# Routed experts by sorted tiles in place of all experts dense, and native fp32 attention projections, in an AdaLN attention and mixture-of-experts block

## The chip, the cores and the metric

The kernel runs on one core of a Trainium2 chip. The metric is the device time of one execution in microseconds. A core has five engines that run side by side, each through its own list of instructions in order, and that wait for each other on semaphores: TensorE (PE, matrix products into PSUM, the weight load shown apart as PEld), VectorE (DVE), ScalarE (ACT), GpSimd (POOL) and SyncE (SP, which here only issues DMAs). Sixteen DMA engines move data between DRAM and SBUF.

## The reference

There are 8 batches of 1024 tokens with 128 features, all fp32. `mod` holds six vectors of 128 for each batch, made from a condition.

```python
h = layernorm(x) * (1 + ca) + sa
q, k, v, g = h @ Wq.T, h @ Wk.T, h @ Wv.T, h @ Wg.T      # 8 heads of 16
q, k = rope(q), rope(k)
kv = einsum('bshd,bshe->bhde', k, v)
num = einsum('bshd,bhde->bshe', q, kv) * scale + v.sum(1)
den = einsum('bshd,bhd->bsh', q, k.sum(1)) * scale + 1024
x = x + ga * (((num / den + conv5(v)) * g) @ Wo.T)
h = layernorm(x) * (1 + cb) + sb
probs = softmax((h @ Wgate + bg) / 5.0)                    # 8 experts
gates = the two largest of probs, each over their sum
out_e = gelu(h @ W1[e] + b1[e]) @ W2[e] + b2[e]            # 128 -> 256 -> 128
x = x + gb * sum_e gates[e] * out_e
```

## The kernel before

Batches are independent. A batch passes through a list of stages (`STAGES`, laid out by `TICK`): norm, transposes of x (`xT`), projections (`qkv`), transposes of v, q and of the inverse denominators, convolution, `gate`, `out`, second norm, `x1T`, `logit`. Its routing follows in `LATE`. Then its experts run as 16 units, one for each half of 512 tokens and each of the 8 experts: every token goes through every expert, and the gate is zero for the six that were not chosen. The schedule has 16 ticks a batch. In each tick one unit of batch f stands beside stages of batch f+1, and every engine walks through the same list (`schedule`, `tick`), so what an engine does next is written out beforehand. The middle six batches are one loop of three rounds with two batches each.

One unit is this chain. `layer1` (L471 to L473): six products 128x128 by 128x512, since each fp32 product is split into three float32r products (`split`: high by high, low by high, high by low). ScalarE applies gelu in PSUM (L702). VectorE multiplies by the gates, which were spread over all partitions through DRAM (L1019). ScalarE rounds to the high part (L709). GpSimd subtracts it for the low part (L807). `layer2` (L592 to L594): six products that accumulate in `ps_y` over all experts. The qkv and gate projections are split in the same way, and their low parts come from GpSimd (L771). `normalise` is L846, the transposes L466, the native fp32 products L502 (kv), L514 (den), L519 (num), L543 (out) and L558 (logit). The bias b2 is one product at L587. SyncE loads x, brings the gates to DRAM and back spread (L400 to L420) and stores y (L428).

## Time and profile before

| | |
|---|---|
| median of 3 runs | 706.93 us (705.43 to 3041.11) |
| span of the profiled execution | 704.5 us |
| PE busy | 590.6 us, 84% |
| PEld busy | 473.8 us, 67% |
| DVE busy | 534.0 us, 76% |
| POOL busy | 450.5 us, 64% |
| ACT busy | 402.9 us, 57% |
| DMA moved | 47.57 MB, mean 68 GB/s |

In rows of groups, `out<-in (partitions x elements, type) xcount` is followed by the busy time in us and the mean ns of one, then by the idle time of the engine just before and what ended it. A native fp32 product has two records on PE, a float32r product or a transpose has one. PE records overlap (the next begins before the last ends), so the pace of a run of products is the distance between their starts. In rows of a stretch the columns are: from and to, length, busy time and number of instructions of PE, PEld, DVE, ACT and POOL, granted TensorE clock as a share of 2.4 GHz, DMA share, GB/s.

### The profile page before, as it was taken

The numbers are of one execution on the slowest core, as the hardware profiler recorded it, in microseconds if no ns is written. First come the engines' busy times: TensorE is split into PE (matmuls) and PEld (weight loads), VectorE is DVE, ScalarE is ACT, GpSimd is POOL, SyncE is SP. The second block draws the span as 40 slices with busy tenths as digits, with TensorE's granted clock in tenths as the row PEclk, the third lists the DMA queues.
The fourth block names the chain that finished last, engine by engine and source line by source line (L and its number), as shares of the span: only waits on it lengthen the run. The fifth ranks groups of instructions, "written<-read, shape, count | busy, mean of one in ns | idle before, by whom it ended". The sixth has DMA issues, their size and how long they took to land.

```text
span 704.5 us, 9302 instructions
## 1 busy us (share of the span) xinstructions
PE 590.6 (84%) x2750; PEld 473.8 (67%) x2750; DVE 534.0 (76%) x1029; ACT 402.9 (57%) x639; POOL 450.5 (64%) x311
## 2 busy tenths in 40 slices
PE   4823897799987988789987989879887989889996
PEld 3623775587776866678765867668665777667884
DVE  5686677977889678787789778796798877884442
ACT  2331565566565746656565746657556655765773
POOL 3372555685866936857667838569458666665885
PEclk9975798899999989989999989999999989998999
DMA  6000341035100441008010341004210180004300
GB/s 239 2 30 0 127 125 31 1 98 168 45 1 15 128 124 45 1 17 247 15 30 14 113 138 45 1 15 158 91 45 0 34 230 15 1 15 169 96 16 15
DMA packets 37682, 47.57 MB, mean 68 GB/s; under 512 B 2096, under 2 KB 20432, under 8 KB 37392
## 3 DMA queue, kind: packets, MB, share of 16 engines
q1 hardware_dynamic: 37216, 46.77, 21.8%
q10 hardware_dynamic: 432, 0.43, 0.2%
q14 instruction: 23, 0.19, 0.1%
q8 instruction: 11, 0.18, 0.1%
HBM read 42.21 MB, written 4.98 MB: 67 GB/s over the span
## 4 chain that ended last, share of the span: by engine, by line
PE 30%; POOL 24%; DVE 21%; issue 17%; ACT 5%; POOLq 1%; DMA 1%; DVEq 0%; SPq 0%; ACTq 0%
POOL hid_l L807 20%; PE ring L466 4%; PE ring L519 3%; DVE xn L846 3%; DVE conv L1005 3%; DVE stats L834 3%; PE ps_y L592 3%; PE ring L514 3%; PE ps_y L593 3%; PE ps_y L594 2%; PE ps_h L471 2%; PE ps_h L472 2%; PE ps_h L473 2%; PE ring L558 2%; DVE hid_g L1019 2%
## 5 line engine op out<-in xcount | busy, mean ns | idle before, releaser
L807 POOL TENSOR_TENSOR hid_l<-hid_g,hid_h 128x1024 fp32r<-128x1024 f32 x128 | 304.9, 2389 | 147.4 <-ACT hid_h L709 138.4
L702 ACT ACTIVATE ps_h<-ps_h,b_f 128x512 f32<-128x512 f32 x256 | 158.5, 658 | 109.0 <-PE ps_h L473 108.3
L1019 DVE TENSOR_TENSOR hid_g<-ps_h,spread 128x1024 f32<-128x1024 f32 x128 | 155.5, 1216 | 71.1 <-POOL hid_l L807 58.2
L709 ACT ACTIVATE hid_h<-hid_g 128x1024 fp32r<-128x1024 f32 x128 | 135.5, 1058 | 11.7 <-DVE hid_g L1019 11.7
L592 PE MATMUL ps_y<-hid_h,w_h 128*128 128x512 f32 x256 | 114.3, 446 | 2.4 <-POOL hid_l L807 2.4
L471 PE MATMUL ps_h<-h_h,w_h 128*128 128x512 f32 x256 | 105.4, 412 | 9.2 <-DVE hid_g L1019 9.2
L593 PE MATMUL ps_y<-hid_h,w_l 128*128 128x512 f32 x256 | 106.0, 414 | 0.0
L594 PE MATMUL ps_y<-hid_l,w_h 128*128 128x512 f32 x256 | 105.8, 413 | 0.0
L472 PE MATMUL ps_h<-h_h,w_l 128*128 128x512 f32 x256 | 102.4, 400 | 0.0
L473 PE MATMUL ps_h<-h_l,w_h 128*128 128x512 f32 x256 | 102.1, 399 | 0.0
L466 PE MATMUL ring<-consts_f,xn 128*128 128x128 f32 x128 | 27.7, 362 | 63.4 <-DVE xn L846 62.2
L466 PEld LDWEIGHTS ring<-consts_f,xn 128*128 128x128 f32 x128 | 19.1, 182 | 73.2 <-DVE xn L846 58.1
L471 PEld LDWEIGHTS ps_h<-h_h,w_h 128*128 128x128 f32 x256 | 49.7, 194 | 24.5 <-DVE hid_g L1019 13.6
L592 PEld LDWEIGHTS ps_y<-hid_h,w_h 128*128 128x128 f32 x256 | 52.9, 207 | 16.0 <-POOL hid_l L807 3.7
L593 PEld LDWEIGHTS ps_y<-hid_h,w_l 128*128 128x128 f32 x256 | 52.0, 203 | 12.8 <-issue 3.0
L594 PEld LDWEIGHTS ps_y<-hid_l,w_h 128*128 128x128 f32 x256 | 51.4, 201 | 12.5
L472 PEld LDWEIGHTS ps_h<-h_h,w_l 128*128 128x128 f32 x256 | 49.4, 193 | 11.1 <-issue 0.2
L473 PEld LDWEIGHTS ps_h<-h_l,w_h 128*128 128x128 f32 x256 | 48.8, 191 | 11.8
L846 DVE TENSOR_SCALAR xn<-x,mean_var,rstd 128x128 f32<-128x128 f32 x64 | 54.7, 924 | 0.1
L776 POOL TENSOR_TENSOR qk<-qk_cos,qk_sin 128x256 f32<-128x256 f32 x64 | 46.7, 746 | 8.5 <-DVE qk_sin L879 8.4
L771 POOL TENSOR_TENSOR h_l<-heads,h_h 128x512 fp32r<-128x512 f32 x16 | 20.6, 1289 | 43.4 <-ACT heads L641 43.2
L1009 DVE SCALAR_TENSOR_TENSOR conv<-v_t,lepe_f,conv 128x1024 f32<-128x1024 f32 x32 | 44.2, 1382 | 0.3
(127 smaller groups left out, 929.9 us busy)
## 6 DMA issues: line engine op xcount, KB each, us to landing
spread<-gates_dram SPq DMA_DIRECT2D x16, 2048.0 KB, 8.9
xs<-in_x SPq DMA_DIRECT2D x8, 512.0 KB, 3.9
out<-y SPq DMA_DIRECT2D x16, 256.0 KB, 2.3
spread<-in_w SPq DMA_DIRECT2D x2, 1024.0 KB, 6.8
gates_e<-parts_dram SPq DMA_DIRECT2D x24, 32.0 KB
ga<-ga_dram SPq DMA_DIRECT2D x1, 512.0 KB, 3.6
spread<-in_wmod SPq DMA_DIRECT2D x1, 384.0 KB, 5.1
spread<-in_wqkvg ACTq DMA_DIRECT2D x1, 256.0 KB, 5.3
```

Source lines behind the costliest of these rows:

```text
L466: last = pe.transpose(dst[:, j * P:(j + 1) * P], src(j), ident)
L471: pe.matmul(dst, wh, ah, start=True, stop=False)
L472: pe.matmul(dst, wl, ah, start=False, stop=False)
L473: return pe.matmul(dst, wh, al, start=False, stop=True)
L592: pe.matmul(ps_y[:, :], w2_h[:, e, g, :], high, start=False, stop=False)
L593: pe.matmul(ps_y[:, :], w2_l[:, e, g, :], high, start=False, stop=False)
L594: last = pe.matmul(ps_y[:, :], w2_h[:, e, g, :], low, start=False, stop=(e == E - 1 and g == HH - 1))
L702: last = act.activation(bank, bank, ACT.Gelu, bias=b1_f[:, e, g:g + 1])
L709: act.activation(hid_h[n % 4][:, :, :], hid_g[n % 2][:, :, :], ACT.Copy)\
L807: pool.tensor_tensor(hid_l[n % 4][:, :, :], hid_g[n % 2][:, :, :], hid_h[n % 4][:, :, :].bitcast(F32), ALU.subtract).then_inc(s_hl, 1)
L846: last = dve.tensor_scalar(xn[:, j, :], src[:, j, :], mean_var[:, j, 0:1], rstd[:, j:j + 1], ALU.subtract, ALU.mult)
L1019: dve.tensor_tensor(hid_g[n % 2][:, :, :], ps_h[n % HIDDEN][:, :, :], gates_all[c][:, e, :].unsqueeze(1).to_broadcast([P, HH, CT]), ALU.mu ...
```

## The change

The experts no longer run dense. For each batch VectorE picks the two experts of each token (`choose`, 13 steps), forms the gates (`soften`, 14 steps) and, with prefix sums from TensorE (nine small float32r products, `prefix`), the row at which each token's copy stands in a list sorted by expert, each expert padded to whole tiles of 128 rows (`put`, 11 steps). There are 2048 copies, and 23 tiles always suffice. GpSimd scatters the normalised rows to DRAM with 16 indirect DMAs of 128 rows (`scat`) and later gathers the results with 16 more (`gat`). SyncE reads each tile's expert number into a register (`value_load`), loads that expert's whole weights for each of the 23 tiles (128 rows of 514 fp32, 263 KB, ring of 8 buffers), loads sorted rows in groups of four tiles (`xg`) and stores results (`ost`). For a tile TensorE transposes the rows (`xsT`), does two native fp32 products 128x128 by 128x128 for layer 1 and two for layer 2. ScalarE moves the transposed group out of PSUM with the modulation, applies gelu (two instructions a tile) and moves out results (`oev`). VectorE combines two gathered rows a token with their gates and the b2 product (`comb`, 16 instructions), then `fin`.

The qkv and gate projections become one native fp32 product each, with no high and low parts. The q and k columns are reordered so that the rotation takes whole halves, with the table repeated over heads (2 MB). The convolution accumulates in `heads` in place, after the division. A batch has 24 ticks (`T`); its own stages stretch from tick -24 (`load`) to 86 (`store_1`), so up to four or five batches are in work at once. The program is written out for all eight batches, with no loop.

```diff
-TICK = {0: [], 1: ["norm1_0", "norm1_1"], 2: ["norm1_apply0", "norm1_apply1", "modulate"],
-        3: ["xT0"], 4: ["xT1", "qkv0"], 5: ["qkv1"], 6: ["qkv2"], 7: ["qkv3"], 8: ["vT"],
-        9: ["kv", "qT", "den_num"], 10: ["rdenT"], 11: ["gate"], 12: ["out0", "out1"],
-        13: ["norm2_apply0", "norm2_apply1"], 14: ["x1T0", "x1T1"], 15: ["logit"]}
...
-SHIFT = 8
-LAG = 3
-Y_TICK = [E * (c + 1) + SHIFT + LAG for c in range(CH)]
...
+T = 24
+FFN = 41
+AT = {"load": -24, "stat1_0": -6, "stat1_1": -5, "pow1": -5, "app1_0": -3, "app1_1": -3, "xT_0": -2, "xT_1": -1,
+      "qkv_0": 0, "qkv_1": 1, "qkv_2": 2, "qkv_3": 3, "vT": 4, "kv": 5, "qT": 5, "den": 6, "dn_0": 7, "dn_1": 7,
+      "conv_0": 8, "conv_1": 9, "conv_2": 10, "conv_3": 11, "gate": 11, "conv_4": 12,
+      "out_0": 13, "out_1": 14, "stat2_0": 15, "stat2_1": 16, "pow2": 16, "app2_0": 17, "app2_1": 18,
+      "x1T_0": 18, "x1T_1": 19, "logit": 20, "choose": 21, "prefix": 22, "soft": 23, "place": 24, "gT": 25}
+AT |= {f"scat_{j}": 28 + j for j in range(J)}
+AT |= {f"w_{t}": FFN + t - 3 for t in range(TILES)}
+AT |= {f"xg_{g}": (FFN - 3 + g if g < 3 else FFN - 1 + GROUP * (g - 3)) for g in range(GROUPS)}
+AT |= {f"xsT_{g}": FFN - 2 + GROUP * g for g in range(GROUPS)}
+AT |= {f"l1_{h}": FFN + 2 * h for h in range(PAIRS)}
+AT |= {f"l2_{h}": FFN + 2 * h + 3 for h in range(PAIRS)}
+AT |= {f"oev_{g}": FFN + GROUP * g + 6 for g in range(GROUPS)}
+AT |= {f"ost_{g}": FFN + GROUP * g + 7 for g in range(GROUPS)}
+AT |= {f"gat_{j}": 70 + j for j in range(J)}
+AT |= {"b2_0": 76, "b2_1": 81, "fin_0": 81, "fin_1": 85, "store_0": 82, "store_1": 86}
+AT |= {f"comb_{j}": 77 + j for j in range(J)}
...
+def schedule(stage):
+    for tick in range(FIRST, T * (B - 1) + LAST + 1):
+        for b in range(B):
+            for name in TABLE.get(tick - T * b, []):
+                kind, _, n = name.partition("_")
+                stage(b, kind, int(n) if n else 0)
...
+                elif kind == "w":
+                    k = nth(b, n)
+                    if n == 0:
+                        sp.wait_ge(s_owner, b + 1)
+                    if k >= W_RING:
+                        old_b, old_t = divmod(k - W_RING, TILES)
+                        sp.wait_ge(s_l2, couple(old_b, old_t // 2) + 1)
+                    e = sp.value_load(owner[b % 2][0:1, n:n + 1], min_val=0, max_val=E - 1)
+                    sp.dma_start(wbuf[k % W_RING][:, :], w_all[bass.ds(e, 1)].rearrange("a p f -> (a p) f"))\
+                        .then_inc(s_wb[k % W_RING], 16)
...
+                elif kind == "xg":
+                    k, first = group(b, n), n * GROUP
+                    many = min(GROUP, TILES - first)
+                    if n == 0:
+                        sp.wait_ge(s_scat[b % 2], 16 * TOP * J * (b // 2 + 1))
+                    if k >= XG_RING:
+                        sp.wait_ge(s_xsT, k - XG_RING + 1)
+                    sp.dma_start(xg[k % XG_RING][:, 0:many, :],
+                                 x_sort[b % 2][first * P:(first + many) * P, :].rearrange("(t p) d -> p t d", p=P))\
+                        .then_inc(s_xg[k % XG_RING], 16)
...
-            def split(dst, wh, wl, ah, al):
-
-                pe.matmul(dst, wh, ah, start=True, stop=False)
-                pe.matmul(dst, wl, ah, start=False, stop=False)
-                return pe.matmul(dst, wh, al, start=False, stop=True)
...
+                        bank_free(f"qkv_{j}", b)
+                        pe.matmul(of(f"qkv_{j}", b)[:, 0:3 * D], h1[i][:, t], wqkvg_f[:, 0:3 * D], start=True, stop=True)\
+                            .then_inc(s_qkv, 1)
...
+                elif kind == "prefix":
+                    if b == 0:
+                        pe.wait_ge(s_tri, 1)
+                    pe.wait_ge(s_route, ROUTE * b + 13)
+                    pe.matmul(pos_ps[:, :], before[:, :], chosen[:, :], start=True, stop=False)
+                    for k in range(1, J + 1):
+                        last = pe.matmul(pos_ps[:, k * E:], every[:, :], chosen[:, 0:(J + 1 - k) * E], start=False,
+                                         stop=(k == J))
+                    last.then_inc(s_pos, 1)
...
+                elif kind == "xsT":
+                    k = group(b, n)
+                    pe.wait_ge(s_xg[k % XG_RING], ring_count(k, XG_RING))
+                    if k >= 1:
+                        pe.wait_ge(s_xs, k)
+                    for t in range(min(GROUP, TILES - n * GROUP)):
+                        last = pe.transpose(ps_x[:, t * P:(t + 1) * P], xg[k % XG_RING][:, t, :], ident)
...
+                elif kind == "l1":
+                    k, g = couple(b, n), group(b, 2 * n // GROUP)
+                    pe.wait_ge(s_xs, g + 1)
+                    if k >= 2:
+                        pe.wait_ge(s_gelu, k - 1)
+                    for m in couple_tiles(n):
+                        w = nth(b, m)
+                        pe.wait_ge(s_wb[w % W_RING], ring_count(w, W_RING))
+                        t = slice(m % GROUP * P, (m % GROUP + 1) * P)
+                        for h in range(HH):
+                            last = pe.matmul(ps_hid[k % 2][:, m % 2, h, :], wbuf[w % W_RING][:, h * P:(h + 1) * P],
+                                             xs_t[g % XS_RING][:, t], start=True, stop=True)
+                    last.then_inc(s_l1, 1)
...
+                elif kind == "l2":
+                    k, g = couple(b, n), group(b, 2 * n // GROUP)
+                    pe.wait_ge(s_gelu, k + 1)
+                    if g >= 1:
+                        pe.wait_ge(s_oe, g)
+                    for m in couple_tiles(n):
+                        w = nth(b, m)
+                        for h in range(HH):
+                            last = pe.matmul(ps_o[:, m % GROUP, :], hid[k % HID_RING][:, m % 2, h, :],
+                                             wbuf[w % W_RING][:, HID + h * D:HID + (h + 1) * D], start=(h == 0),
+                                             stop=(h == HH - 1))
+                    last.then_inc(s_l2, 1)
...
+                elif kind == "l1":
+                    k = couple(b, n)
+                    act.wait_ge(s_l1, k + 1)
+                    if k >= HID_RING:
+                        act.wait_ge(s_l2, k - HID_RING + 1)
+                    for m in couple_tiles(n):
+                        w = wbuf[nth(b, m) % W_RING]
+                        for h in range(HH):
+                            last = act.activation(hid[k % HID_RING][:, m % 2, h, :], ps_hid[k % 2][:, m % 2, h, :],
+                                                  ACT.Gelu, bias=w[:, 2 * HID + h:2 * HID + h + 1])
+                    last.then_inc(s_gelu, 1)
...
+                elif kind == "scat":
+                    if n == 0:
+                        pool.wait_ge(s_slot, b + 1)
+                        if b == 0:
+                            pool.wait_ge(s_zero, 16 * 2 * GROUPS)
+                        if b >= 2:
+                            pool.wait_ge(s_xsT, group(b - 1, 0))
+                    for k in range(TOP):
+                        at = slots[b % 4][:, k * J + n:k * J + n + 1]
+                        pool.indirect_dma_start(x_sort[i], bass.IndirectOffsetOnAxis(ap=at, axis=0), xn2[i][:, n, :],
+                                                None).then_inc(s_scat[i], 16)
+                elif kind == "gat":
+                    if n == 0:
+                        for r in range(O_RING):
+                            pool.wait_ge(s_os[r], 16 * len(range(r, group(b + 1, 0), O_RING)))
+                        if b >= 1:
+                            pool.wait_ge(s_comb, J * b)
+                    for k in range(TOP):
+                        at = slots[b % 4][:, k * J + n:k * J + n + 1]
+                        pool.indirect_dma_start(og[:, k, n, :], None, o_sort[i],
+                                                bass.IndirectOffsetOnAxis(ap=at, axis=0)).then_inc(s_gat[n], 16)
...
+                step(b, 4, dve.scalar_tensor_tensor(key[:, :, :], below[:, :, :], 0.0, by_tile(rev), ALU.is_ge, ALU.mult))
+                step(b, 5, dve.tensor_reduce(key_top[:, :], key[:, :, :], AX_X, ALU.max))
+                hot0, hot1 = (hot[:, k, :].rearrange("p (j e) -> p j e", e=E) for k in range(TOP))
+                step(b, 6, dve.tensor_tensor(hot0, key[:, :, :], by_expert(key_top[:, :]), ALU.is_equal))
+                step(b, 7, dve.scalar_tensor_tensor(logit[:, :, :], hot0, FAR, below[:, :, :], ALU.mult, ALU.add))
+                step(b, 8, dve.tensor_reduce(top[:, :], logit[:, :, :], AX_X, ALU.max))
+                step(b, 9, dve.tensor_tensor(logit[:, :, :], logit[:, :, :], by_expert(top[:, :]), ALU.subtract))
...
+            def put(b):
+                dve.wait_ge(s_pos, b + 1)
+                many = pos_ps[:, J * E:(J + 1) * E].unsqueeze(2).to_broadcast([P, E, E])
+                step(b, 28, dve.tensor_tensor(over[:, :, :], many, steps.unsqueeze(1).to_broadcast([P, E, E]), ALU.is_gt))
+                step(b, 29, dve.tensor_reduce(n_tiles[:, :], over[:, :, :], AX_X, ALU.add))
+                step(b, 30, dve.tensor_tensor(over[:, :, :], lower, n_tiles[:, :].unsqueeze(1).to_broadcast([P, E, E]),
+                                              ALU.mult))
+                step(b, 31, dve.tensor_reduce(base[:, :], over[:, :, :], AX_X, ALU.add))
+                step(b, 32, dve.scalar_tensor_tensor(place[:, :].rearrange("p (j e) -> p j e", e=E), by_tile(base[:, :]),
...
-            def low_part(f, n):
-                pool.wait_ge(s_hh, f.count(UNITS, n + 1))
-                if not (f.first and n < 4):
-                    pool.wait_ge(s_l2, f.count(UNITS, n - 3))
-                pool.tensor_tensor(hid_l[n % 4][:, :, :], hid_g[n % 2][:, :, :],
-                                   hid_h[n % 4][:, :, :].bitcast(F32), ALU.subtract).then_inc(s_hl, 1)
...
-            def gate_hidden(f, n):
-                c, e = divmod(n, E)
-                if e == 0:
-                    dve.wait_ge(s_gall[c], f.count(16, 16))
-                dve.wait_ge(s_gelu, f.count(UNITS, n + 1))
-                if not (f.first and n < 2):
-                    dve.wait_ge(s_hl, f.count(UNITS, n - 1))
-                dve.tensor_tensor(hid_g[n % 2][:, :, :], ps_h[n % HIDDEN][:, :, :],
-                                  gates_all[c][:, e, :].unsqueeze(1).to_broadcast([P, HH, CT]),
-                                  ALU.mult).then_inc(s_hg, 1)
...
+                elif kind == "comb":
+                    c = n // JC
+                    dve.wait_ge(s_gat[n], 16 * TOP * (b + 1))
+                    if n % JC == 0:
+                        dve.wait_ge(s_b2, CH * b + c + 1)
+                    g = gate2[b % 4]
+                    dve.scalar_tensor_tensor(u[:, n, :], og[:, 0, n, :], g[:, 0, n:n + 1],
+                                             ps_z[:, n % JC * D:(n % JC + 1) * D], ALU.mult, ALU.add).then_inc(s_fin, 1)
+                    dve.wait_ge(s_fin, (J + CH) * b + c * (JC + 1) + n % JC + 1)
+                    dve.scalar_tensor_tensor(u[:, n, :], og[:, 1, n, :], g[:, 1, n:n + 1], u[:, n, :], ALU.mult, ALU.add)\
+                        .then_inc(s_comb, 1)
+                elif kind == "fin":
+                    dve.wait_ge(s_comb, J * b + (n + 1) * JC)
...
```

## Rows read from the trace of the kernel before

**Rows 1.** Busy time by stretch, three batches: busy us (instructions), clock, DMA share, GB/s.
```profile
300.00:382.00 82.00, 72.56 (x343) 58.90 (x344) 67.36 (x132) 49.38 (x79) 55.32 (x39) 0.92 0.23 66
...
464.00:546.00 82.00, 71.53 (x345) 57.89 (x346) 68.69 (x132) 49.14 (x79) 54.87 (x39) 0.94 0.21 66
```

**Rows 2.** Groups by line and form: busy us, mean ns, idle before, releaser.
```profile
L807 POOL TENSOR_TENSOR hid_l<-hid_g,hid_h 128x1024 fp32r<-128x1024 f32 x128 | 304.9, 2389 | 147.4 <-ACT hid_h L709 138.4 <-PE ps_y L594 8.5
L702 ACT ACTIVATE ps_h<-ps_h,b_f 128x512 f32<-128x512 f32 x256 | 158.5, 658 | 109.0 <-PE ps_h L473 108.3
L1019 DVE TENSOR_TENSOR hid_g<-ps_h,spread 128x1024 f32<-128x1024 f32 x128 | 155.5, 1216 | 71.1 <-POOL hid_l L807 58.2 <-issue 6.4 <-ACT ps_h L702 5.3
...
L846 DVE TENSOR_SCALAR xn<-x,mean_var,rstd 128x128 f32<-128x128 f32 x64 | 54.7, 924 | 0.1
```

**Rows 3.** Waits: engine and line, what it waited for, us, times, longest.
```profile
POOL hid_l L807 <- ACT hid_h L709: 138.4, 52, 12.4
...
DVE hid_g L1019 <- POOL hid_l L807: 58.2, 44, 2.3
```

**Rows 4.** Timeline of TensorE, one stretch: start us, us, line, op, count.
```profile
233.09 0.34 PE L471 MATMUL ring<-wqkvg_h,h_h 128*128 128x384 f32 x1
233.27 0.34 PE L472 MATMUL ring<-wqkvg_h,h_l 128*128 128x384 f32 x1
...
234.14 0.40 PE L592 MATMUL ps_y<-hid_h,w_h 128*128 128x512 f32 x1
234.37 0.39 PE L593 MATMUL ps_y<-hid_h,w_l 128*128 128x512 f32 x1
...
243.03 1.95 PE L502 MATMUL ring<-v,qk 128*128 128x129 f32 x16
244.81 1.04 PE L466 MATMUL ring<-consts_f,qk 128*128 128x128 f32 x8
```

**Rows 5.** Group by form, the wide native fp32 product.
```profile
L519 PE MATMUL ring<-xn,kv_s 128*128 128x512 f32 x32 | 26.1, 966 | 0.0
```

**Rows 6.** Busy time by stretch, while L519 runs.
```profile
580.00:584.00 4.00, 4.00 (x7) 1.93 (x8) 3.51 (x5) 1.81 (x3) 0.00 (x0) 0.50 0.05 17
```

**Rows 7.** Timeline of VectorE, first batch's routing and second's norm.
```profile
60.63 0.22 DVE L947 TENSOR_TENSOR logit<-ring,br_f 128x64 f32<-128x64 f32 x1 [2.96 <-PE ring L558]
60.89 0.22 DVE L952 TENSOR_REDUCE top<-logit 128x8 f32<-128x64 f32 x1
...
67.11 2.14 DVE L846 TENSOR_SCALAR xn<-xs,mean_var,rstd 128x128 f32<-128x128 f32 x8
```

**Rows 8.** Timeline of TensorE, first batch's first projection.
```profile
15.21 0.66 PE L471 MATMUL ring<-wqkvg_h,h_h 128*128 128x384 f32 x1 [2.14 <-POOL h_l L771]
```

**Rows 9.** Groups by form, smaller work of VectorE, GpSimd and ScalarE.
```profile
L1009 DVE SCALAR_TENSOR_TENSOR conv<-v_t,lepe_f,conv 128x1024 f32<-128x1024 f32 x32 | 44.2, 1382 | 0.3
L758 POOL TENSOR_TENSOR rstd<-var_eps,minus_half 128x4 f32<-128x4 f32 x32 | 33.2, 1037 | 2.5
...
L878 DVE TENSOR_TENSOR qk_cos<-ring,rope_f 128x256 f32<-128x256 f32 x64 | 26.7, 418 | 8.7 <-PE ring L473 7.2 <-POOL qk L776 1.2
...
L771 POOL TENSOR_TENSOR h_l<-heads,h_h 128x512 fp32r<-128x512 f32 x16 | 20.6, 1289 | 43.4 <-ACT heads L641 43.2
...
L646 ACT ACTIVATE v<-ring 128x128 f32<-128x128 f32 x64 | 17.4, 279 | 37.5 <-DVE qk_sin L879 37.2
```

**Rows 10.** Busy time by stretch, a 2 MB load and a 0.5 MB load.
```profile
153.00:162.00 9.00, 9.00 (x48) 7.80 (x47) 6.13 (x11) 6.30 (x12) 9.00 (x10) 1.00 0.78 240
188.00:192.00 4.00, 4.00 (x18) 3.22 (x18) 3.96 (x12) 3.42 (x5) 3.32 (x4) 1.00 0.47 133
```

**Rows 11.** DMA issues: count, KB each, us from issue to landing.
```profile
spread<-gates_dram SPq DMA_DIRECT2D x16, 2048.0 KB, 8.9
...
out<-y SPq DMA_DIRECT2D x16, 256.0 KB, 2.3
```

**Rows 12.** Timeline of SyncE's queue, one DMA issue.
```profile
187.80 0.39 SPq L395 DMA_DIRECT2D xs<-in_x  x1
```

1355 lines of the change are left out of this document (543 added, 812 removed).

## The prediction

> **What bounds the kernel now.** I read the stretches first, to see what one batch costs in the steady part: two of three successive stretches of 82 us stand here, with nearly equal instruction counts, so a batch takes 82 us [rows 1]. Then the groups by form: the expert unit owns the top of every engine [rows 2]. GpSimd's L807 takes 2.39 us for each of 16 units, 38 us a batch. Then the waits: L807 waits for ScalarE's rounding, and VectorE's L1019 waits for L807 [rows 3]. So the unit's chain through four engines is tight, while TensorE is the fullest. Its real load is read from distances between starts in its timeline [rows 4]: 0.233 us for a split product of 512 columns, 0.18 us for one of 384, 1.78 us for eight native products of 129 columns (0.2225 us each, 1.72 ns a column), 0.13 us for a transpose. A batch has 192 + 6 of the first (46.1 us), 24 of the second (4.3), 48 transposes (6.2), four runs of eight native products (kv, den, out, logit, 7.1) and L519 (26.1 us over 8 batches, 3.3) [rows 5]. Together 67 us of 82: TensorE is filled to 0.82, at a clock of 0.92 to 0.94 of 2.4 GHz [rows 1].
>
> **What the change removes and adds, for one batch in the steady part.**
>
> TensorE. Out go the 192 + 6 + 24 split products, 50.4 us. In come 92 native products of 128 columns for the experts, 92 x 0.2225 = 20.5 us, 16 more transposes net (64 x 0.13 = 8.3 us in all), and wide native products: qkv 8 x 384, and num, gate and b2 with 6 x 512 columns, 6144 columns. I price them by the 129-column row, 10.6 us. The other bound is L519, a 512-column native product in 1.63 us (3.19 ns a column), which would give 19.6 us; but it ran at a granted clock of 0.50, the lower of the two levels [rows 6], after waits. The nine small prefix products I price as transposes, 1.2 us. With the four runs of eight (7.1) the sum is 47.7 us, 57 by the other bound. So the projections themselves gain little on TensorE (5.7 us before against 7.0); the gain there is on the engines that made the parts. By the Trainium skill ("FP8 and Floating Point Precision", TensorE Precision Notes) true fp32 is four passes through the array; the 1.72 ns a column agrees with four at 2.4 GHz, and the sum by it would be the same.
>
> VectorE. Out go the 16 gatings, 16 x 1.22 = 19.5 us [rows 2], and the dense ranking. It gets 38 routing steps at 0.26 us (start to start of two such steps) [rows 7], 9.9 us, and 16 combining operations. The norm's 16 operations cost 0.855 us each in the one group, beside GpSimd's long subtractions [rows 2], and 0.27 us where GpSimd was quiet [rows 7]. I take 0.27: 4.3 us. 128-column work counts the same, so combining is 4.3 and the statistics 4.3 + 1. Rotation is 16 x 0.418, the convolution 5 x 1.38 [rows 9]; ten operations of 512 columns I interpolate at 0.7 us; small ones 1.5. Sum 46 us.
>
> ScalarE. 46 gelus and 8 copies at 0.28 us, 23.5 operations of 512 columns at 0.66 us [rows 2, 9]: 31 us. Not the bound.
>
> GpSimd. The 38 us of L807 and the low parts of h (L771, 2.6 us) go. Two powers (1.04 us) with their additions, 2.6 us, and four qk additions of 512 columns at 1.29 us [rows 9], 5.2 us, stay. New are 32 indirect DMAs, and no row shows one. From below: a DMA issue from SyncE holds its queue 0.39 us [rows 12]. From above: the longest GpSimd instruction, 2.39 us [rows 2]. Building 128 addresses in software is nearest to the power, 1.04 us for a tiny operand, plus reading the indices, so I take 1.25 us, 40 us a batch, and the engine's sum is 48 us (20 and 84 at the ends). By the Trainium skill ("DMA: Bandwidth & Descriptors", Latency and other measured facts) the first byte of a software-built DMA comes after about 1 us; as the price of one, an estimate, that would make the sum 40 us.
>
> SyncE and the DMA engines. A batch now moves 23 x 0.263 MB of weights, 1.5 MB of sorted rows in, 1.5 MB of results out, 2.1 MB through the indirect DMAs and 1 MB of x and y: 12.1 MB. The DMA engines moved 240 GB/s at a share of 0.78 and 133 at 0.47 [rows 10], some 300 GB/s when full, whether the rows were 2 KB or 512 B. That is 40 us of 64, so the traffic hides, and it is a bit over twice today's, 66 GB/s for 82 us [rows 1]. SyncE has 38 issues at 0.39 us, 15 us, and 23 register loads of unknown cost: from 0 up to a whole landing, 2.3 us [rows 11]. It stays under 64 us up to 2.1 us a load; I take that it is covered by the two to three ticks of lead.
>
> So four resources stand at 40 to 48 us. The steady period follows in two ways. First, TensorE's 47.7 us at the same filling of 0.82 gives 58 us. Second, I walk the 24 ticks and add the longer of VectorE and TensorE in each: projections and rotation 11, v and kv 6, den and the division 8, convolution with combining 10, out, second norm and its statistics 11, transposes, logit and first norm's statistics 5, choosing and applying the first norm 5, gates 4: 60 us. Some twenty hand-overs from engine to engine in it, exposed by about 0.2 us each, add 4. I take **64 us**, and the spread is 56 to 72.
>
> **The span.** The first batch took from 15.2 us (first projection) to 60.6 us (logit) [rows 7, 8]. Without the contended norm (8 x 0.59 = 4.7 us) and about 1 us of parts, 40 us stay; VectorE now does the modulation in front of the first statistics, 5 us later, so the logits come at 60 us. Routing to the slots takes 32 steps and the prefix, 9 us, then the exposed 16 scatters 20 us, a landing and the first sorted load 2.3 us each [rows 11], transposing and evacuating 1 us, on which the first layer 1 starts (tick 41) at 95, with rounding 97 us. The second batch's attention lies beside it. From tick 41 to 193, where the last attention ends, 152 ticks x 64/24 = 405 us. Then 44 ticks hold only expert tiles: 0.39 MB a tile at 300 GB/s is 1.3 us, TensorE 1.1, so 1.45 us, 64 us. At the end come 16 gathers (20 us), a landing (2.3), combining and finishing (2) and the store (2.3): 27 us. Sum 593 us against the span of 704.5. The median of the runs lies 2.4 us above the span, so **595 us**.
>
> **Rivals.** *GpSimd becomes the bound* (slower side). Each indirect DMA beyond 1.76 us makes the period 8 + 32c, larger than 64; the 0.5 us more lengthens the exposed scatters and gathers by 16 us to 611. Each further 0.1 us adds 3.2 us to 6.3 periods and to the ends, 23 us. From 2.24 us the kernel is slower by 2%; at 2.39 us it takes about 758. For it: nothing here shows the price, and the qk additions stand behind ten gathers in GpSimd's list, with TensorE's kv and VectorE behind them. Against it: every small GpSimd operation seen is near 1 us [rows 9]. VectorE's norm and GpSimd also exclude each other: 0.855 against 0.27 us [rows 2, 7]; if GpSimd must wait out the 16 norms, that is 4.3 us a batch more, 52 us, still under 64. By the Trainium skill ("SBUF — State Buffer", SBUF: two separate sides) such operations also keep GpSimd from writing descriptors; by that the sum would be these 52 us.
>
> *DMA or SyncE bounds.* If latency and mixed reads and writes hold the engines to 160 GB/s, a batch takes 76 us: 12 x 6.3 more, 670 us. Against it: a share of 0.8 was held for 9 us [rows 10].
>
> *The lower clock.* TensorE is filled less evenly, and stretches of tiny products and waits have already been followed by a clock of 0.50 [rows 6]. If half of its work ran there, its load would be 72 us, at 0.82 a period of 87: 740 us.
>
> **Chances.** Forecast 0.55; GpSimd 0.20, of which 0.13 beyond 2.24 us; DMA or SyncE 0.15; clock 0.10, half of it slower. With 2% as what a measurement of this kernel can tell: faster 0.77 (0.55, 0.05 of GpSimd, 0.15, 0.02), same 0.05, slower 0.18. The forecast alone spans 56 to 72 us a period, 544 to 646. The range takes in the DMA rival and GpSimd's up to 2.2 us at the top (715), and at the bottom cheap indirect DMAs of 0.4 us (13 us less at either end): 530.
>
> **What the profile would show.** TensorE's pace by starts near 48 us a batch; VectorE's norm at 0.27 us; GpSimd's indirect DMAs around 1.25 us apart; equal stretches of about 64 us; DMA share near 0.6; first layer 1 at 97 us; a tail of 27 us after the last expert tile. The prediction is wrong if the scatters or gathers come 2 us apart, if SyncE waits at the register loads, or if the chain of waits lies on the attention's stages with all engines half idle, which would mean that the exposed hand-overs are more than 4 us.

## The result and the profile after

The changed kernel took 790.56 us (median of 4 runs, 788.8 to 793.14) beside 706.18 us for the kernel before: a ratio of 1.1199, with a 95% interval of 1.1133 to 1.1264. It is 12% slower, where 595 us had been predicted with a range up to 715. On two other chips the same kernel later took 662 and 661 us, 6% faster than before. What follows takes the two gaps apart: 595 to 662, and 662 to 790. The chips are called R (this result), B, C, D, E and F in what follows; R may be one of the others, the runs don't say. The kernel before took 703 to 706 us (medians) in every group of runs.

First the page of the changed kernel on chip R: span, busy time by engine, clock.

```profile
span 789.3 us, 9804 instructions
...
PE 495.7 (63%) x2808; PEld 403.6 (51%) x2808; DVE 352.1 (45%) x1151; ACT 244.7 (31%) x661; POOL 321.3 (41%) x325
```

Then the stretches that answer to [rows 1], in the same columns.

```profile
300.00:382.00 82.00, 54.86 (x324) 45.39 (x323) 40.43 (x134) 27.90 (x73) 37.58 (x38) 0.80 0.49 136
464.00:546.00 82.00, 55.08 (x315) 44.32 (x314) 38.46 (x118) 28.79 (x77) 35.02 (x35) 0.80 0.49 136
```

TensorE had 72 us in such a stretch and has 55 now, VectorE 67 and now 40 (a batch takes 88.8 us on this chip, so that 82 us are no longer a whole one). The work went away as forecast, yet no engine is near full. The chain of waits names something that the kernel before did not have (by engine, then by line):

```profile
PE 23%; another core or an unknown queue 21%; DVE 19%; issue 15%; ACT 8%; POOL 6%; DMA 6%; SPq 2%; POOLq 0%; ACTq 0%; DVEq 0%
```

Only one core runs, so 21% of the span is time for which the trace has no releaser. The waits say who stands there (engine and line, what it waited for, us, times, longest):

```profile
PEld bank L378 <- issue: 95.6, 14, 13.0
...
DVE den L774 <- remote: 64.6, 6, 17.9
...
ACT hid L562 <- remote: 57.0, 7, 13.8
DVE u L814 <- remote: 38.4, 1, 38.4
ACT xs_t L552 <- remote: 35.9, 6, 16.7
```

Everyone who waits for "remote" here reads a product of TensorE: `den` is L367's, `hid` L442's, `xs_t` L430's, `u` reads L460's. (Of the 38.4 us of `u`, only the last 11 are of this kind: L460 is over at 725.4 us and `u` starts at 736.5. Before that it waits for expert tiles, as on other chips.) The timeline beside the second batch's scatters, which run from 141 to 161 us, shows the place. The attention in it is the third batch's:

```profile
149.21 1.92 PE L367 MATMUL bank<-ksum_s,q_t 128*128 128x8 f32 x16 [2.90 <-issue]
150.28 0.96 POOL L619 DMA_INDIRECT x_sort<-xn,slots  x1 [0.30 <-issue]
...
151.46 1.76 PE L442 MATMUL ps_hid<-xs_t,wbuf 128*128 128x128 f32 x8
151.54 0.96 POOL L619 DMA_INDIRECT x_sort<-xn,slots  x1 [0.30 <-issue]
...
153.01 1.91 PE L373 MATMUL bank<-q_t,kv_s 128*128 128x512 f32 x2
...
160.40 0.95 POOL L619 DMA_INDIRECT x_sort<-xn,slots  x1 [0.30 <-issue]
164.07 0.23 DVE L774 TENSOR_SCALAR den<-bank 128x64 f32<-128x64 f32 x1 [17.92 <-remote]
```

TensorE's records say that the eight tiny products of `den` were over at 151.1 us. Their semaphore rises at 164.05 in the trace's list of semaphore events, 13 us later and 2.7 us after the last of the 16 scatters has ended, and VectorE starts 0.02 us after that. In the first batch's series (81 to 102 us) `den` is still read 0.04 us after its last product. From the second batch's series on it is read 6 to 13 us late in every batch, and the products of the expert tiles (`hid`, `xs_t`) up to 19 us late, while GpSimd issues scatters back to back. In the series of gathers there is less of it. Completions of VectorE and ScalarE are prompt as their readers show: ScalarE starts 0.03 us after `rden` in all eight batches, and TensorE 0.05 us after ScalarE. In the kernel before, each of TensorE's completions stands in the list of semaphore events within 0.02 us of the end of its record.

The list of events has a second mark of it. On chip R it lacks 142 of VectorE's 771 completions, 48 of ScalarE's 370 and 47 of TensorE's 489, most of them during the series, and none of GpSimd's. The changed kernel's trace lacks 4 on chip F and 2 on chip B, and the kernel before lacks one. The runs on chips C and D, which show the lateness below, lack events as well. So events of every engine but GpSimd are missing there, while the readers of VectorE and ScalarE named above are not held up.

The trace doesn't tell whether the products themselves are held up or only the news of them, since the ends of TensorE's records are modelled. It does tell that TensorE hears others at once. In the next batch's series VectorE's `den` ran at 237.25, ScalarE followed at 238.10, and TensorE's L378, which waits for that, stands at 238.78.

### The profile page after: what moved, and what is told of

It is laid out like the page before. It is cut to its first block, busy times and chain, and to the rows that moved or that the text cites. A ratio compares the mean times of both kernels' runs of the same rounds, so it can differ in the third digit from the quotient of the medians.

```text
span 789.3 us, 9804 instructions
## 1 busy us (share of the span) xinstructions
PE 495.7 (63%) x2808; PEld 403.6 (51%) x2808; DVE 352.1 (45%) x1151; ACT 244.7 (31%) x661; POOL 321.3 (41%) x325
## 4 chain that ended last, share of the span: by engine, by line
PE 23%; another core or an unknown queue 21%; DVE 19%; issue 15%; ACT 8%; POOL 6%; DMA 6%; SPq 2%; POOLq 0%; ACTq 0%; DVEq 0%
PE ps_o L453 5%; DVE heads L740 5%; PE ps_hid L442 5%; ACT hid L562 4%; PE bank L340 4%; POOL og L629 3%; DMA wbuf<-in_w_all 3%; PE bank L353 2%; POOL qk L603 2%; DMA xg<-x_sort 1%; DVE xn L650 1%; ACT o_s L570 1%; DVE stats L639 1%; PE ps_x L430 1%
## 5 line engine op out<-in xcount | busy, mean ns | idle before, releaser
L629 POOL DMA_INDIRECT og<-o_sort,slots x128 | 122.7, 959 | 117.6 <-DMA o_sort<-o_s 69.2
L562 ACT ACTIVATE hid<-ps_hid,wbuf 128x128 f32<-128x128 f32 x368 | 105.6, 370 | 207.0 <-PE ps_hid L442 130.6
L453 PE MATMUL ps_o<-wbuf,hid 128*128 128x128 f32 x736 | 119.9, 315 | 56.5 <-ACT o_s L570 33.4
L453 PEld LDWEIGHTS ps_o<-wbuf,hid 128*128 128x128 f32 x736 | 109.0, 226 | 73.4 <-ACT hid L562 71.3
L619 POOL DMA_INDIRECT x_sort<-xn,slots x128 | 125.6, 981 | 39.8 <-issue 38.4
L442 PE MATMUL ps_hid<-xs_t,wbuf 128*128 128x128 f32 x736 | 119.9, 310 | 20.2 <-DMA wbuf<-in_w_all 15.5
L442 PEld LDWEIGHTS ps_hid<-xs_t,wbuf 128*128 128x128 f32 x736 | 108.3, 222 | 33.3 <-DMA wbuf<-in_w_all 17.5
L603 POOL TENSOR_TENSOR qk<-qk_cos,qk_sin 128x512 f32<-128x512 f32 x32 | 40.8, 1275 | 92.0 <-DVE qk_sin L763 91.2
L378 PE MATMUL bank<-consts_f,qk 128*128 128x128 f32 x64 | 15.7, 392 | 97.8 <-ACT heads L532 56.3
L378 PEld LDWEIGHTS bank<-consts_f,qk 128*128 128x128 f32 x64 | 10.5, 199 | 116.5 <-issue 95.6
L340 PE MATMUL bank<-wqkvg_f,h 128*128 128x384 f32 x128 | 55.7, 569 | 1.6 <-ACT v L508 1.5
L740 DVE SCALAR_TENSOR_TENSOR heads<-v_t,lepe_f,heads 128x1024 f32<-128x1024 f32 x40 | 51.2, 1281 | 0.5
L762 DVE TENSOR_TENSOR qk_cos<-bank,rope_f 128x256 f32<-128x256 f32 x64 | 26.9, 420 | 29.7 <-PE bank L340 24.9
L430 PE MATMUL ps_x<-consts_f,xg 128*128 128x128 f32 x184 | 32.5, 303 | 7.7 <-DMA xg<-x_sort 7.7
L460 PE MATMUL ps_z<-b_f,gates_t 64*128 64x512 f32 x32 | 23.6, 825 | 20.0 <-DVE u L817 15.1
L394 PE MATMUL bank<-wo_g,heads 128*128 128x128 f32 x128 | 22.6, 337 | 20.6 <-issue 13.4
```

Source lines behind the costliest of these rows:

```text
L340: pe.matmul(of(f"qkv_{j}", b)[:, 0:3 * D], h1[i][:, t], wqkvg_f[:, 0:3 * D], start=True, stop=True)\
L378: last = pe.transpose(of(f"rden_{n}", b)[:, j * P:(j + 1) * P], rden_x[:, k:k + HEADS, :].rearrange("p h d -> p (h d)"), ident)
L430: last = pe.transpose(ps_x[:, t * P:(t + 1) * P], xg[k % XG_RING][:, t, :], ident)
L442: last = pe.matmul(ps_hid[k % 2][:, m % 2, h, :], wbuf[w % W_RING][:, h * P:(h + 1) * P], xs_t[g % XS_RING][:, t], start=True, stop=True)
L453: last = pe.matmul(ps_o[:, m % GROUP, :], hid[k % HID_RING][:, m % 2, h, :], wbuf[w % W_RING][:, HID + h * D:HID + (h + 1) * D], start=(h ...
L562: last = act.activation(hid[k % HID_RING][:, m % 2, h, :], ps_hid[k % 2][:, m % 2, h, :], ACT.Gelu, bias=w[:, 2 * HID + h:2 * HID + h + 1])
```

## The experiments

**Is it what GpSimd issues?** The first four runs were on chip B. The first is a measurement by itself: TensorE runs 24 groups in each phase, ScalarE reads each group.

```diff
+pe.wait_ge(s_act, c - 5)        # six groups in flight
+... 4 transposes, or 4 native 128-column products, or 8 products of 8 columns, then then_inc(s_pe, 1)
+pool.indirect_dma_start(rows, IndirectOffsetOnAxis(ap=at, axis=0), src[:, n, :], None)   # x16 in its phase
```

> None of the reference is computed here; this is a measurement by itself. TensorE runs the same 24 groups (four 128-column transposes, four native fp32 128-column products, eight products of 8 columns, each group read by ScalarE) in eight phases, while beside it stands: nothing; 16 indirect scatters from GpSimd; 16 indirect gathers; 16 plain transfers issued by GpSimd; 16 tensor operations of 128x512 on GpSimd and no transfer; 16 plain transfers issued by SyncE; 16 scatters with a tensor operation after each; nothing again. Theory (TensorE's completions are seen late while GpSimd issues indirect transfers back to back): the two empty phases and the SyncE phase have equal length, some 25 to 35 us, and the scatter and gather phases are longer by 10 to 20 us each, with completions up to 13 to 20 us late in them. Rival 1 (the traffic itself, or the DMA queues, delay them): the two phases with plain transfers are as long as those with indirect ones. Rival 2 (a busy GpSimd of any kind delays them): the tensor phase is longer as well. Rival 3 (what is late in the whole kernel has nothing to do with GpSimd): all eight phases agree within 2 us.

Rival 3 came out: no completion was late. The phases lasted 26.4, 34.8, 25.1, 25.1, 31.6, 25.1, 41.1 and 29.6 us. The 34.8 us of the scatters go with a granted clock of 0.71, the 31.6 and 29.6 with 0.78 and 0.85, and the 41.1 are GpSimd's own work.

The other three change the kernels:

```diff
-pool.indirect_dma_start(x_sort[i], IndirectOffsetOnAxis(ap=at, axis=0), xn2[i][:, n, :], None)
+pool.dma_start(x_sort[i][(k * J + n) * P:(k * J + n + 1) * P, :], xn2[i][:, n, :])
```

> The changed kernel, in which each of the 32 indirect transfers of a batch is a plain one of the same 128 rows of 512 bytes, still issued by GpSimd at the same place. It leaves the sorting out: the rows go to, and come from, linear places. Theory (only indirect transfers, back to back, hold up TensorE's completions): 600 to 650 us. Rival (any transfer built by GpSimd does it): 760 to 800 us. Rival (traffic to and from DRAM is the bound): 770 to 800 us as well.

Measured: 620.79 us (611.32 to 622.69), a ratio of 0.8718 (0.8641 to 0.8796). No wait is put down to "remote".

> The changed kernel with the same plain transfers issued by SyncE in the same ticks, so that GpSimd issues none; bytes, rows and DRAM places are those of the run beside it. It leaves the sorting out. Theory (what GpSimd issues holds up TensorE's completions, some 20 us of each 88 us batch): steady period 64 to 70 us, 600 to 650 us in all. Rival (DRAM traffic and its small rows are the bound): 770 to 800 us. Rival (the lower clock, 0.79, is the cause and not the result): the clock stays under 0.82 and the time over 740 us.

Measured: 625.4 us, ratio 0.8846 (0.8797 to 0.8896), clock 0.873. The same bytes in rows of the same size, though in linear places, cost no 790 us on this chip, so neither traffic nor SyncE's register loads account for such a time.

> The kernel before with the second part of the change alone: projections of q, k, v and the gate as one native fp32 product each, in place of three products of split halves; everything is computed. By the prediction's prices the qkv products of a batch go from 8 x 1.95 to 8 x about 2.05 us of TensorE and the gate's from 2 x 1.04 to 2 x 1.04, so TensorE gains nothing, while ScalarE and GpSimd lose two operations each of 128x512 for both halves: 690 to 706 us. If instead the native products are what slowed the changed kernel, 720 to 760 us.

The diff is the change's own second part. Measured: 698.65 us, ratio 0.9859 (0.9788 to 0.9929): a small gain, and the native products are not what slowed the changed kernel.

At this point the gap between 621 and 790 seemed to be what indirect transfers cost. That comparison was flawed, since the two numbers came from different chips, and I had not run the changed kernel beside them. It took until the fifteenth run to see it.

**Which transfers?** The next four were on chip C.

```diff
-at = slots[b % 4][:, k * J + n:k * J + n + 1]
+at = lin[:, k * J + n:k * J + n + 1]          # a constant table that counts up
```

> The changed kernel with all 32 indirect transfers of a batch, but their row numbers come from a constant table that counts up (row j x 128 + partition), so no sorting is done; each transfer writes or reads the same 128 consecutive rows as the plain ones did at 621 us. Theory (an indirect transfer as such holds up TensorE's completions): 770 to 800 us, with waits of TensorE's consumers as in the changed kernel. Rival (it is the scattered addresses in DRAM): 610 to 640 us.

Measured: 796.5 us, with the same waits. So scattered addresses are not needed for it.

> The changed kernel with its 16 scatters a batch indirect and its 16 gathers plain (so the outputs of the experts come back from linear places; the sorting is left out on that side). Theory (long back-to-back series do the harm, and the scatters are the series of 14 to 16): most of the 170 us between plain and indirect stays, 720 to 760 us. Rival (scatters and gathers cost alike, by their number): 700 to 710 us.

Measured: 677.21 us.

> The changed kernel with its 16 gathers a batch indirect and its 16 scatters plain (the tokens go to linear places; the sorting is left out on that side). Theory (long back-to-back series do the harm; the gathers come 6 and then 2 at a time, except in the last batches): 640 to 680 us. Rival (scatters and gathers cost alike, by their number): 700 to 710 us.

Measured: 689.65 us. Both expectations missed: the gathers, 6 and then 2 at a time, cost as much as the scatters, and either alone costs far less than both. Neither the changed kernel nor one with plain transfers alone ran on chip C, so what each costs can't be said to the microsecond. The waits of the run with indirect scatters show that its lateness is there, but less:

```profile
ACT hid L562 <- remote: 48.4, 5, 13.4
...
DVE u L812 <- remote: 24.8, 5, 6.1
...
DVE den L772 <- remote: 18.1, 1, 18.1
```

`den` is late there only once, by 11 us, in the one series (144 to 164 us) in which scatters follow one another with nothing between. In the later series plain gathers stand among the scatters, and `den` is read after 0.04 us.

The fourth is the measurement by itself with two groups in flight and with company:

```diff
-pe.wait_ge(s_act, c - 5)
+pe.wait_ge(s_act, c - 1)
+dve.tensor_tensor(tc, ta, tb, ALU.add)         # 12 of 128x1024 in some phases
+sp.dma_start(big[k % 4], w[n % 8])             # 12 loads of 512 KB in some phases
```

> None of the reference is computed: a second measurement of the cost by itself, nearer to the kernel. TensorE now waits for ScalarE's reading of the group before last, and ten phases stand beside: nothing; 16 scatters to consecutive rows; 16 scatters to random rows; scatters with a busy VectorE (128x1024); scatters with 12 loads of 512 KB by SyncE; scatters with 512-column products in the groups; random scatters with all three; random gathers with all three; plain transfers with all three; and all three with no transfer of GpSimd. Theory (indirect transfers beside some load hold up TensorE's completions): one of the loaded scatter phases is longer than the last phase by 5 to 20 us, and names the company that it takes; the plain phase is as long as the last. Rival (what is late in the kernel needs something that no probe has, such as TensorE's own waits on several engines): the seventh, eighth, ninth and tenth phases agree within 2 us.

The phases lasted 19.8 us (nothing), 29.0 (scatters), 29.3 (random rows), 29.7 (with VectorE), 34.6 (with loads), 35.8 (wide products), 34.3 (all three), 33.7 (gathers with all three), 22.7 (plain with all three) and 26.1 (no transfer, all three). The granted clock was 1.00 with nothing and 0.65 with scatters, so part of the 9 us between them is the clock that fell with the waits. So the lateness can be had without the kernel, scatters alone suffice, random rows add nothing (29.3 against 29.0), and plain transfers built by the same engine don't do it. Its row in the waits:

```profile
ACT back L99 <- remote: 82.2, 14, 13.8
```

**What does it need?** The next run was on chip D. It varies the gap between transfers, the groups in flight, what TensorE does meanwhile, and the rows of a transfer.

> None of the reference is computed: a third measurement of the cost by itself. Twelve phases of 24 groups on TensorE, beside 16 transfers of GpSimd each: none; scatters back to back; scatters with one 128x512 tensor operation of GpSimd after each; with three; scatters with 4 and with 6 groups of TensorE in flight in place of 2; scatters with 8 transposes that nobody waits for after each group; scatters of 32 rows in place of 128; the same tensor operations without transfers; plain transfers; scatters with 1 group in flight; none again. Theory (a completion of TensorE comes late when TensorE stands waiting at a semaphore while GpSimd builds an indirect transfer, as the run with 2 groups in flight showed and the one with 6 did not): the second phase is 8 to 12 us longer than the first or last, the one with 1 group in flight at least as much, those with 6 groups and with filling transposes no longer than their own work; with gaps the delay falls with the share of time in which transfers are built, to under half with three operations. Rival (the number of rows sets it): 32 rows cost a quarter or less of 128. Rival (the depth makes no difference and the first measurement missed it by chance): 4 and 6 in flight are late as well.

GpSimd marks the start of each phase; the distance of two marks is the length of a phase.

```profile
20.67 0.20 POOL L102 TENSOR_TENSOR gc<-ga,gb 128x8 f32<-128x8 f32 x1 [20.22 <-DMA out<-src]
47.63 0.20 POOL L102 TENSOR_TENSOR gc<-ga,gb 128x8 f32<-128x8 f32 x1 [26.76 <-PE bank L75]
96.74 0.20 POOL L102 TENSOR_TENSOR gc<-ga,gb 128x8 f32<-128x8 f32 x1 [28.71 <-PE bank L75]
...
218.59 0.20 POOL L102 TENSOR_TENSOR gc<-ga,gb 128x8 f32<-128x8 f32 x1
260.17 0.20 POOL L102 TENSOR_TENSOR gc<-ga,gb 128x8 f32<-128x8 f32 x1 [21.31 <-PE bank L75]
305.06 0.19 POOL L102 TENSOR_TENSOR gc<-ga,gb 128x8 f32<-128x8 f32 x1 [24.61 <-PE bank L75]
363.54 0.19 POOL L102 TENSOR_TENSOR gc<-ga,gb 128x8 f32<-128x8 f32 x1 [38.21 <-PE bank L75]
417.62 0.20 POOL L102 TENSOR_TENSOR gc<-ga,gb 128x8 f32<-128x8 f32 x1 [35.34 <-PE bank L75]
```

Nothing: 27.0 us. Scatters back to back: 49.1. Not all of that is late completions. When the last scatter ends, 21 us into the phase, 7 of 24 groups have been read, where the first phase had read 18; two more follow at 70.7 us. After that nothing is late any more, but the granted clock is 0.59 (1.00 in the first phase), and the other 15 groups take 26 us. With a tensor operation after each, ScalarE's last read in the phase is at 122.38:

```profile
122.38 0.23 ACT L88 ACTIVATE back<-bank 128x64 f32<-128x64 f32 x1 [1.46 <-PE bank L75]
```

That is 25.6 us after the mark at 96.74: no delay at all (GpSimd's own list runs on to 136 us). With three operations it is 27.2. Four groups in flight take 41.6 us, six 44.9, so depth is no cure and that part of my theory fell. With the filling transposes the phase lasts 58.5 us, in which single waits of up to 12 us are seen, so filling is no cure either. Transfers of 32 rows take 54.1, at a clock of 0.59, with a single wait of 12.5 us in them, so the number of rows doesn't set it. Operations alone take 25.7, plain transfers 27.3, one group in flight 68.0, and nothing again 35.3, at a lower clock. On this chip each back-to-back phase is slow, and no phase with an operation between transfers is.

**Does a short operation cure the kernel?** The next two were on chip E.

```diff
 pool.indirect_dma_start(...)
+pool.wait_ge(s_pad, pads[0])
+pool.tensor_tensor(pad[:, 2, :], pad[:, 0, :], pad[:, 1, :], ALU.add).then_inc(s_pad, 1)   # 8 or 128 columns
```

> The changed kernel, everything computed, with one GpSimd operation of 128x8 (about 0.2 us) put behind each indirect transfer, so that no two of them follow one another directly. It adds 32 operations, 6 to 8 us of GpSimd, to a batch. Theory (it is transfers back to back that hold up TensorE's completions, as the measurement by itself shows: 49.1 us without and 25.6 us with a 128x512 operation between): steady period 64 to 72 us, 600 to 660 us in all, if so short an operation is enough. Rival (the length of the gap matters, and 0.2 us is too short): 760 to 800 us. Rival (in the whole kernel something else makes the completions late): as before, 785 to 800 us.

Measured: 686.94 us, ratio 0.9755 (0.969 to 0.982), with no wait for "remote". The upper end of what was expected is missed by 27 us.

> The same with an operation of 128x128 (about 0.4 us) behind each indirect transfer. It adds 12 to 15 us of GpSimd to a batch, which then has 61 to 65 us of work. Theory: 610 to 670 us, near GpSimd's own bound. Rival (the gap has to be as long as a 128x512 operation, 1.3 us): still 720 to 790 us. If this one is at 620 us and the shorter gap at 790 us, the length of the gap decides.

Measured: 733.36 us, ratio 1.0403 (1.0358 to 1.0447). More GpSimd work between transfers makes it slower, so here GpSimd's own time counts.

**What is left, 687 against 621?** The next three were on chip B.

> The changed kernel with a 128x8 operation of GpSimd behind each indirect transfer, and the addition that ends the rotation of q and k (four of 128x512 a batch, 1.28 us each on GpSimd) moved to VectorE; everything is computed. Theory (the walk of a batch is held where this addition waits in GpSimd's order behind gathers: from the transposes of v to the kv products lie 5.8 us, beside 1.8 us with plain transfers, and 0.8 us at each of the four ticks before): the period falls from 73.5 to 67 to 70 us, 645 to 670 us in all. Rival (those additions are hidden and the period is set by something else): 680 to 695 us.

```diff
-pool.tensor_tensor(qk[:, 2 * n:2 * n + 2, :], qk_cos[n % 2][:, :, :], qk_sin[n % 2][:, :, :], ALU.add)
+dve.tensor_tensor(qk[:, 2 * n:2 * n + 2, :], qk_cos[n % 2][:, :, :], qk_sin[n % 2][:, :, :], ALU.add)
```

Measured: 646.02 us (644.51 to 647.57), ratio 0.9166 (0.9105 to 0.9228). That is 41 us less than the same kernel with the additions on GpSimd takes on this chip (686.67 us, below). The four additions are 5.1 us a batch, but they only pay because they stood in front of something, as the section below shows.

> The changed kernel with plain transfers, which leaves the sorting out, and an operation of 128x224 behind each, so that each transfer takes as long of GpSimd as an indirect one with its 128x8 operation, about 1.4 us. Theory (what is left between 621 us with plain transfers and 687 us is GpSimd's own time in the order of the walk): 675 to 700 us. Rival (something else of indirect transfers is left, such as their landing or the DRAM rows): 621 to 640 us.

Measured: 695.72 us, ratio 0.9892 (0.9814 to 0.9971), inside what was expected. But the run was not what it was meant to be. Its lines, and the convolution in the changed kernel on the same chip:

```profile
L604 POOL TENSOR_TENSOR pad<-pad 128x224 f32<-128x224 f32 x256 | 181.5, 709 | 5.6
L630 POOL DMA_DIRECT2D x_sort<-xn x128 | 71.5, 558 | 4.0 <-DVEq L733 4.0
L750 DVE SCALAR_TENSOR_TENSOR heads<-v_t,lepe_f,heads 128x1024 f32<-128x1024 f32 x40 | 68.8, 1721 | 0.5
```

```profile
L740 DVE SCALAR_TENSOR_TENSOR heads<-v_t,lepe_f,heads 128x1024 f32<-128x1024 f32 x40 | 51.2, 1281 | 0.5
```

A transfer with its operation takes 1.2 us from start to start, less than an indirect one by itself (1.27) and not the 1.4 that was meant. And the operation of 224 columns makes VectorE slower: a convolution step takes 1.72 us in place of 1.28, and VectorE is busy for 432 us in place of 352. So the 696 us are GpSimd's and VectorE's together, and that they come near 687 says nothing of either. The rival, that something else of indirect transfers is left, is not settled by this run.

> None of the reference is computed: eleven phases of 24 groups on TensorE with two groups in flight. Beside them: 128x8 operations alone; 16 scatters back to back; scatters with a 128x8 operation after each; after every second; after every fourth; scatters that each wait for their landing; gathers back to back; gathers with an operation after each; scatters back to back again; scatters with a wait after each that has long been met; operations alone again. Theory (an operation of GpSimd's engine between transfers lets the completions through): about 26 us for each phase with an operation or a landing after each transfer, 40 to 60 us for those back to back, gathers as well as scatters, with single gaps of up to 6 us where only every second or fourth has one; a met wait changes nothing. Rival (the time between transfers counts, whatever fills it): the phase that waits for landings is free of it, and the one with a met wait is not, so it would look the same; the phase with every second operation would then stand half way.

The marks of the first back-to-back phase and its neighbours:

```profile
52.46 0.20 POOL L100 TENSOR_TENSOR gc<-ga,gb 128x8 f32<-128x8 f32 x1 [28.04 <-PE bank L75]
78.15 0.20 POOL L100 TENSOR_TENSOR gc<-ga,gb 128x8 f32<-128x8 f32 x1 [5.29 <-PE bank L75]
106.99 0.20 POOL L100 TENSOR_TENSOR gc<-ga,gb 128x8 f32<-128x8 f32 x1 [6.43 <-PE bank L75]
```

Both theories missed. Sixteen scatters back to back took 25.7 us here, and every phase took 25.7 to 32.6 us but the one that waits for landings, where GpSimd took 42 and ScalarE was done after 25.6. The instructions of the back-to-back phase are those that took 49.1 us on chip D. So this run says nothing on what ends a lateness. It says that chip B has none.

**Is it the chip?** The changed kernel and the one with short operations, both unchanged, on chip B:

> The changed kernel itself once more, everything computed, beside the run with short operations between the transfers on the same chip. Theory 1 (back-to-back indirect transfers hold up TensorE's completions on every chip, and the probes without it were chance): 785 to 800 us. Theory 2 (it depends on the chip, as the probes suggest): 785 to 800 us on a chip that has it, 660 to 700 us with no completion late by more than 1 us on a chip that has not.

Measured: 662.11 us (658.1 and 666.12), ratio 0.9388 (0.9252 to 0.9524). Theory 2 holds: the kernel that took 790 us takes 662 here, and `den` is read 0.04 us after its last product in all eight batches.

> The changed kernel with a 128x8 operation of GpSimd behind each indirect transfer, on the same chip as the changed kernel itself. Theory (the operation ends the lateness wherever it occurs): 680 to 695 us, also where the changed kernel takes 790 us. Rival (the earlier run was on a chip that has no lateness, and the operation does nothing): the same time as the changed kernel beside it, plus up to 15 us.

Measured: 686.67 us (682.02 and 691.31). The rival's case, though with more than its 15 us: on this chip the operation costs 25 us and brings nothing.

The last two ran on chip F:

> The changed kernel itself as witness for the chip, everything computed. On a chip with late completions 785 to 800 us, on one without 655 to 670 us; a time in between would say that the lateness comes and goes on one chip.

Measured: 661.43 us (660.79 and 662.06), ratio 0.9375 (0.9301 to 0.9448).

> The version with a 128x8 operation behind each indirect transfer and the rotation's addition on VectorE, everything computed, beside the witness. Theory (the operation ends the lateness wherever it occurs): 640 to 655 us on any chip. Rival (the operation does nothing, and the lateness belongs to the chip): 640 to 655 us where the witness takes 660 us, 740 to 780 us where the witness takes 790 us.

Measured: 639.54 us (637.38 and 641.7), ratio 0.9064 (0.8965 to 0.9164). Chip F has no lateness either, so what this run was for stays open: the cure has been seen at work in the measurement by itself on chip D, and not in the whole kernel on a chip that needs it.

The page of the changed kernel on chip F, its stretch that answers to [rows 1], and two waits:

```profile
span 660.2 us, 9804 instructions
...
PE 473.8 (72%) x2808; PEld 391.5 (59%) x2808; DVE 352.6 (53%) x1151; ACT 241.8 (37%) x661; POOL 337.9 (51%) x325
```

```profile
300.00:382.00 82.00, 62.99 (x387) 52.88 (x387) 52.52 (x163) 30.92 (x87) 49.38 (x45) 0.90 0.61 172
```

```profile
DVE den L774 <- PE bank L367: 21.8, 8, 3.1
...
PEld bank L378 <- issue: 16.5, 15, 2.2
```

The busy times of VectorE and ScalarE are those of chip R within 1.2% (352.6 against 352.1, 241.8 against 244.7). What went is VectorE's wait at L774 (64.6 us to "remote" there, 21.8 to TensorE here, at most 3.1 at a time) and TensorE's at L378 (95.6 against 16.5). The clock follows: 0.86 over the run against 0.79.

## Why the prediction was wrong, step by step

**Prices.** These held. GpSimd's indirect transfer, taken at 1.25 us between bounds far apart, has starts 1.27 us apart and these means on chip R:

```profile
L619 POOL DMA_INDIRECT x_sort<-xn,slots x128 | 125.6, 981 | 39.8 <-issue 38.4 <-DVEq L723 1.4
L629 POOL DMA_INDIRECT og<-o_sort,slots x128 | 122.7, 959 | 117.6 <-DMA o_sort<-o_s 69.2 <-issue 47.6
```

VectorE's norm runs at 0.27 us (eight in 2.14 us), as in [rows 7] and not as in [rows 2]. The wide native products go by the 129-column row: two of 384 columns in 1.46 us. The DMA engines moved 172 GB/s at a share of 0.61 on chip F, in line with [rows 10]. SyncE's register loads were nearly covered: TensorE's waits for weights come to 18.5 us over the whole run there. The power was mis-sized (1.65 us of 128x8 elements against 1.04 of 128x4), 1.2 us a batch. VectorE's long operations do make a scatter longer, 1.9 and 1.5 us beside the convolution on chip B, and L619 has a mean of 1.11 us on F; on R, where VectorE stood still, 0.98. The Trainium skill ("SBUF — State Buffer", SBUF: two separate sides) says that VectorE can hold a port pair that it shares with GpSimd, and that GpSimd can't write the descriptors of a DMA meanwhile. The longer scatters agree with that, but no run here shows that the port is the reason. The size here, 0.13 us in the mean and 2 us a batch, didn't decide.

**The span.** The starts at which the sum was cut, on chip F (first layer 1, last transposed gates, the last run of layer 2):

```profile
111.88 1.01 PE L442 MATMUL ps_hid<-xs_t,wbuf 128*128 128x128 f32 x3 [0.87 <-ACT xs_t L552]
...
553.85 0.42 PE L423 MATMUL ps_z<-consts_f,gates 128*64 128x128 f32 x1
...
629.19 1.57 PE L453 MATMUL ps_o<-wbuf,hid 128*128 128x128 f32 x12 [1.29 <-ACT o_s L570]
```

With the last product at 630.5 us:

| term | forecast | chip F | chip R |
|---|---|---|---|
| start to tick 41 | 97 | 111.9 | 107.5 |
| 152 ticks | 405 | 441.9 | 562.6 |
| expert tiles alone | 64 | 76.7 | 89.5 |
| tail | 27 | 29.7 | 29.7 |
| span | 593 | 660.2 | 789.3 |

*Start to tick 41, 15 us on F.* The step that failed is "The second batch's attention lies beside it", which put that attention at nothing. The text followed only the first batch, with "Routing to the slots takes 32 steps and the prefix, 9 us, then the exposed 16 scatters". The slots were ready at 73.4 us, 4 us after the forecast. Then, in GpSimd's list, the second batch's four additions stand ahead of the first scatter:

```profile
76.16 1.27 POOL L603 TENSOR_TENSOR qk<-qk_cos,qk_sin 128x512 f32<-128x512 f32 x1 [15.34 <-DVE qk_sin L763]
...
83.19 1.27 POOL L603 TENSOR_TENSOR qk<-qk_cos,qk_sin 128x512 f32<-128x512 f32 x1 [1.07 <-DVE qk_sin L763]
84.65 1.20 POOL L619 DMA_INDIRECT x_sort<-xn,slots  x1 [0.18 <-issue]
```

The scatters began 11 us after their data. The prediction named "qk additions behind ten gathers" and did not look at what stands before the scatters. But that is the smaller part, for earlier scatters help little. With plain transfers on chip B the last one ends at 92.9 us and not at 104.7, and the first layer 1 (L442) moves only from 110.1 to 108.5 us:

```profile
103.02 3.78 PE L394 MATMUL bank<-wo_g,heads 128*128 128x128 f32 x16 [6.18 <-DVE heads L786]
106.60 1.06 PE L430 MATMUL ps_x<-consts_f,xg 128*128 128x128 f32 x4
108.53 2.08 PE L442 MATMUL ps_hid<-xs_t,wbuf 128*128 128x128 f32 x8 [0.87 <-ACT xs_t L552]
```

TensorE takes the sorted rows (L430) right behind the second batch's `out` (L394), which stands ahead of them in its list and had waited 6.2 us for VectorE's convolution. On F, too, the version with the additions on VectorE begins its scatters ten microseconds earlier, at 74.6 us, and reaches layer 1 at 108.6 us in place of 111.9. So some 3 us of the 15 are the additions, and 12 are the second batch's attention up to `out`. The prediction had what it takes to see this: its own prices for those stages (11, 6, 8 and 10 us) make 35 us behind the slots, which gives 104 us and not 95.

*The steady period, 37 us on F.* Forecast 64 us, measured 441.9 x 24 / 152 = 69.8. The step that failed is the walk, "the longer of VectorE and TensorE in each" tick: GpSimd was left out of it. In ticks with two gathers and an addition GpSimd needs 2 x 1.27 + 1.28 = 3.8 us, against some 2.7 us a tick, and the kv products wait for the last addition. From chip B, the transposes of v and then the kv products, first with indirect and then with plain transfers:

```profile
201.66 1.04 PE L347 MATMUL bank<-consts_f,v 128*128 128x128 f32 x8
...
206.67 3.81 PE L353 MATMUL bank<-v,qk 128*128 128x129 f32 x16 [3.07 <-POOL qk L603]
```

```profile
399.95 1.04 PE L347 MATMUL bank<-consts_f,v 128*128 128x128 f32 x8
...
401.71 1.95 PE L353 MATMUL bank<-v,qk 128*128 128x129 f32 x16
```

5.0 us lie between them in the one and 1.8 in the other. The period, reckoned in the same way, tells how much of the miss this is. On chip B it is 70.5 us for the changed kernel, 65.8 with plain transfers and 65.7 with none from GpSimd; on F it falls from 69.8 to 64.8 with the additions on VectorE. So about 5 of the 5.8 us a batch, some 30 of the 37, are GpSimd's place in the walk, and without it the forecast of 64 was close. On chip B the time rises with GpSimd's time from one transfer's start to the next: 621 us at 0.53 us, 662 at 1.27, 687 at 1.38. (The 696 us of the plain transfers with their long operation don't belong in this row, since VectorE was slower there.) That is the rival "GpSimd becomes the bound" at work far below the 1.76 us from which I let it begin: an engine needn't be full to hold the walk, it is enough that its work stands in front in the same tick.

*Expert tiles alone, 13 us, and the tail, 3.* These were mis-sized: 1.74 us a tick and not 1.45. The forecast let the DMA engines move 300 GB/s there, and they moved 215, at a share of 0.76. No run tests what held them or the tail.

Together the four parts make the 67 us from 593 to 660. This part of the miss lies inside the range given.

**From 660 to 789.** 129 us, of which 121 are in the 152 ticks, where the period is 88.8 us and not 69.8. The step that failed is "Some twenty hand-overs from engine to engine in it, exposed by about 0.2 us each, add 4": on chip R the hand-overs from TensorE took up to 19 us each during the series of transfers, and the period grew by 19 us. No rival of the prediction has it either. The text said that the prediction would be wrong "if the chain of waits lies on the attention's stages with all engines half idle"; it does, but at TensorE's completions alone and by 6 to 19 us at a time. Part of the 129 us is the lower clock that goes with the waits: TensorE is busy for 495.7 us on R and 473.8 on F with the same products. Shown: on chips R, C and D completions come late in the series of indirect transfers without anything between (the changed kernel on R, three kernels and a measurement by itself on C, a measurement by itself on D), on B and F they don't (the changed kernel on both, two measurements by themselves on B). Shown on D, by itself: one GpSimd operation between transfers ends it. Shown on C: plain transfers of GpSimd don't do it, and scattered addresses are not needed. The cause itself stays open. Not shown: what differs between the chips, whether the products or only their signals are late, whether the recording of the trace, which lacks events on just these chips, has a part in it, and whether the short operation cures the whole kernel on R, C or D.

**The other rivals.** DMA or SyncE as the bound: not at 662 or 790 us, since the same bytes with the same register loads take 621 and 625 us on chip B. The lower clock: on chip R it is 0.79 and TensorE is filled by 63%, but the stalls are there first and the clock rises where they are missing. It follows and doesn't lead, though it lengthens what it follows. The low bound of 530 needed cheap transfers, which there are not.

**The change's two parts.** The native projections alone bring 1.4% (698.65 us). With the experts by sorted tiles, the new schedule and the reordered rotation and convolution it is 6% together where completions are prompt, minus 12% where they are not; no run takes these apart. With the additions on VectorE and a short operation behind each transfer it is 8% to 9% (646 and 640 us), the best version run here that does the sorting. The same without the short operation, which cost 25 us on chip B, was not run.

## What to carry to other kernels

Walk a schedule with every engine in it, the half-idle ones too: what stands ahead of an instruction in its own queue delays it, however empty the engine is, and that holds for the next batch's work ahead of the first batch's as well. A control that stands in for an engine's time must be read in the trace before it is believed: here it slowed a second engine. A comparison between versions needs the reference version in the same group of runs; here a figure taken over from another chip misled the study for a dozen runs. And where a kernel issues indirect transfers in series, look for waits of TensorE's consumers that the trace can't put down to anyone, and put another operation between the transfers if they are there.

## What the runs showed of the hardware

- The same kernel takes 790 us on one chip and 661 to 662 on two others, while the kernel before takes 703 to 706 us on all of them. The time of the kernel before doesn't give the difference away.
- A GpSimd indirect transfer of 128 rows of 512 bytes holds its engine for 0.96 to 0.98 us and 0.30 us of gap, whether it gathers or scatters, whether the rows are in order or not. A plain one takes 0.55 us.
- On chips that show it, TensorE's completions come up to 19 us late while such transfers are issued back to back. A measurement by itself took 49.1 us in place of 27.0, some of it at the lower clock that followed, also with 32 rows each (54.1 us), and not with one 128x512 operation of GpSimd after each (25.6 us).
- The trace itself marks such a chip: it lacks 237 of 1630 completions of VectorE, ScalarE and TensorE in the run of 789 us, and 2 and 4 in the traces of the same kernel on chips B and F.
- A scatter beside VectorE's 128x1024 convolution step takes 1.5 to 1.9 us in place of 0.97. A 128x224 operation of GpSimd between plain transfers makes the same step of VectorE 1.72 us long in place of 1.28.
